# Two blocks of experts and attention on one core: expert chunks cut in halves, value groups without a product of zeros, and a new table of stages

## The reference

```
# block 1
nx = layer_norm(x)                                  # [2,512,128]
w  = softmax(nx @ Wq @ (ctx @ Wk).T * 128**-0.5)    # over 77 context rows
ev = w @ (ctx @ Wv)                                 # "evidence"
comb = concat([nx, ev, cond])                       # 384 wide
p  = softmax(comb @ router_W + router_b)            # 3 experts
h  = silu(comb @ e_w1 + e_b1)                       # 3 experts x 256
routed = sum_e p[e] * (h[e] @ e_w2[e] + e_b2[e])
g  = sigmoid(silu(comb @ gate_w1 + gate_b1) @ gate_w2 + gate_b2)
x  = x + g * (routed @ out_w + out_b)
# block 2, 16 heads of 8 channels, six vectors of cond modulate it
x = x + gate_msa * (self_attention(modulated layer_norm(x)) @ self_o_w + b)
x = x + cross_attention(layer_norm(x), ctx) @ cross_o_w + b
x = x + gate_mlp * (gelu(modulated layer_norm(x) @ mlp_w1 + b) @ mlp_w2 + b)
```

## Time and profile before

| | |
|---|---|
| median of three runs | 314.41 us (312.88 to 314.87) |
| the profiled execution | 312.69 us, span 310.9 us |
| TensorE busy | 259.0 us, 1804 instructions |
| VectorE busy | 173.3 us |
| ScalarE busy | 148.9 us |
| GpSimd busy | 46.1 us |
| mean granted TensorE clock | 0.912 |

### The profile page before, as it was taken

One profiled execution on the slowest core, in us unless ns is written; L12 is line 12 of the kernel. 1 busy time (PEld: TensorE's weight loads), 2 busy tenths in 40 slices (PEclk: granted clock), 3 DMA queues, 4 the chain that ended last, 5 costly groups with the idle time before them and its releaser, 6 DMA issues.

```text
span 310.9 us, 4809 instructions
## 1 busy us (share of the span) xinstructions
PE 259.0 (83%) x1804; PEld 144.4 (46%) x1804; DVE 173.3 (56%) x387; ACT 148.9 (48%) x274; POOL 46.1 (15%) x58
## 2 busy tenths in 40 slices
PE   3779988988557799897989899899899975778786
PEld 2665647446402343343434434354445543457356
DVE  6744224752894878776977874797432534052221
ACT  1213214443002466764855658648877643524442
POOL 1300391183012800000100001001010002000110
PEclk9999999999955789999999999999999997556759
DMA  6969930006440165100021000300002100300000
GB/s 179 407 100 193 175 64 0 2 28 172 149 134 2 47 173 142 50 4 2 0 61 44 2 6 15 91 4 5 2 2 71 51 3 4 98 3 21 2 0 34
DMA packets 15460, 19.72 MB, mean 63 GB/s; under 512 B 3237, under 2 KB 13477, under 8 KB 14445
## 3 DMA queue, kind: packets, MB, share of 16 engines
q1 hardware_dynamic: 15437, 19.42, 23.6%
HBM read 16.19 MB, written 3.03 MB: 62 GB/s over the span
## 4 chain that ended last, share of the span: by engine, by line
PE 47%; ACT 9%; DVE 9%; issue 4%; POOL 0%; ACTq 0%; DVEq 0%; POOLq 0%
PE ps L1141 42%; ACT region L745 6%; DVE neg_max L1019 3%; PE ps L1414 3%; DVE neg_max L1028 2%; ACT pv_sb L754 1%; PE ps L1169 1%; ACT nT L648 1%; PE ps L1425 1%; DVE normed L844 1%; PE ps L1353 1%; DVE max_parts L1047 1%; ACT L745 0%; POOL rstd L542 0%; DVE max_parts L1045 0%
## 5 line engine op out<-in xcount | busy, mean ns | idle before, releaser
L745 ACT ACTIVATE region<-ps 128x512 f32<-128x512 f32 (+1 forms) x160 | 86.7, 595 | 43.5 <-PE ps L1141 42.2
L1019 DVE TENSOR_REDUCE neg_max<-ps 128x2 f32<-128x1024 f32 x64 | 76.5, 1220 | 23.6 <-PE ps L1141 23.0
L1141 PE MATMUL ps<-k_room,Qs 128*128 128x512 bf16 x128 | 41.1, 412 | 6.5 <-DVE neg_max L1019 5.6
L1141 PE MATMUL ps<-Qs,k_room 128*128 128x256 bf16 x256 | 42.5, 279 | 4.1 <-ACT region L745 2.5
L542 POOL TENSOR_TENSOR rstd<-var_eps,minus_half 128x2 f32<-128x2 f32 (+1 forms) x12 | 9.7, 811 | 211.6 <-DVE var_eps L833 211.6
L1141 PE MATMUL ps<-region,V 128*32 128x256 f32 x512 | 39.5, 390 | 0.0
L1141 PEld LDWEIGHTS ps<-Qs,k_room 128*128 128x128 bf16 x256 | 20.2, 99 | 28.7 <-ACT region L745 17.0
L1141 PEld LDWEIGHTS ps<-k_room,Qs 128*128 128x128 bf16 x128 | 10.9, 102 | 21.4 <-issue 9.8
L678 ACT ACTIVATE region<-ps,hidden_b 128x512 f32<-128x512 f32 x14 | 9.5, 686 | 21.0 <-PE ps L1141 21.0
L1028 DVE TENSOR_REDUCE neg_max<-ps 128x8 f32<-128x616 f32 x16 | 12.2, 794 | 12.7 <-PE ps L1141 12.5
L1141 PEld LDWEIGHTS ps<-region,V 128*32 128x32 f32 x512 | 10.8, 108 | 17.2 <-issue 11.7
(11 more groups left out here) (159 smaller groups left out, 338.0 us busy)
## 6 DMA issues: line engine op xcount, KB each, us to landing
Qs<-q_scr SPq DMA_DIRECT2D x24, 192.0 KB
k_room<-k_scr SPq DMA_DIRECT2D x4, 576.0 KB
k_room<-in_pad SPq DMA_DIRECT2D x2, 896.0 KB
Qs<-in_pad SPq DMA_DIRECT2D x4, 448.0 KB
q_scr<-q_parts SPq DMA_DIRECT2D x8, 192.0 KB, 2.1
region<-in_w_hidden SPq DMA_DIRECT2D x1, 1344.0 KB, 9.4
w_attn<-in_w_attn SPq DMA_DIRECT2D x1, 896.0 KB, 14.1
k_scr<-k_parts SPq DMA_DIRECT2D x2, 384.0 KB, 2.5
```

The costliest lines, as they stand in the source:

```text
L745: nc.scalar.activation(probs[0:rows_, s % UNITS, j0:j0 + CT // 2, :], ps[0:rows_, EXP0 + e % 2, :].rearrange("p (j n) -> p j n", n=TU), AC ...
L1019: nc.vector.tensor_reduce(neg_max[:, b, t, h:h + MH], ps[:, bank:bank + MH, :], axis=AX, op=ALU.max, negate=True).then_inc(max_read, 1)
L1141: return nc.tensor.matmul(out, lhsT, rhs, start=start, stop=stop)
```

## The change

Three edits. First, `hidden_layer` of TensorE becomes two functions and two stages: `hidden_x:b.c` issues the product of the normalized input, `hidden:b.c` adds the evidence. The table places three `hidden_x` of the first sequence around `scores:1`, ahead of the first softmax's normalization. Second, a value group of the self attention has no product of zeros; its first value product (first key tile, first half of the heads) carries the start flag, and all others add. Third, the whole table `ORDER` is new (471 words). A stage `warm` and its function are added, too, but the table has none, and the four counts in `START_WARM` are zero, so no instruction comes of it. The memset of the zeros moves to the front of VectorE's instructions.

```
-scores:0 bias:0 scores_norm:0 scores_T:0 scores:1 evidence:0 bias:1 route:0 route_norm:0 hidden:0.0 scores_norm:1
+scores:0 hidden_x:0.0 scores:1 hidden_x:0.1 scores_norm:0 hidden_x:0.2 scores_T:0 bias:0 scores_norm:1 bias:1
...
+            def keep_warm(bank, n):
+
+                claim(bank)
+                for _ in range(n):
+                    mm(ps[:, bank, :], spread(zero16[:, :]), zero16[:, :].to_broadcast([P, T]))
...
-            def hidden_layer(b, c):
+            def hidden_input(b, c):
                 bank = HID0 + c % 4
+                if c == 0:
+                    pe.wait_ge(hidden_in, 16)
+                    pe.wait_ge(nT_ready, b + 1)
                 claim(bank)
                 mm(ps[:, bank, :], hidden_w(c, 0), nT[b][:, :], stop=False)
+
+            def hidden_evidence(b, c):
+                bank = HID0 + c % 4
+                if c == 0:
+                    pe.wait_ge(ev_ready, b + 1)
                 mm(ps[:, bank, :], hidden_w(c, 1), evT[b], start=False).then_inc(hid_raw, 1)
                 read_by(bank, hid_ready, HC * b + c + 1)
...
                     claim(PVB)
-                    if kind == "self":
-
-                        mm(ps[:, PVB, :], spread(zero16[:, :]), zero16[:, :].to_broadcast([P, T]), stop=False)
...
-                        last = mm(out_, V[b][:, kt, VS * h:VS * h + 32], probs[:, s % UNITS, j, :], start=False,
+                        last = mm(out_, V[b][:, kt, VS * h:VS * h + 32], probs[:, s % UNITS, j, :], start=kt == 0 and r == 0,
                                   stop=final)
```

More of the change, by code:

```diff
@@ new lines @@
+weights:1 hidden:0.4 scores_T:1 expert_bias:0 weights:2 hidden_x:0.5 fold:0 fold:1 hidden_x:0.6 hidden:0.5
+hidden:0.6 evidence:1 route:1 expert:0.0 expert:0.1 gate:0 expert:0.2 expert:0.3 gated:0 hidden_x:1.0 stats:1.0
+add_bias:self.1 hidden:1.0 hidden_x:1.1 hidden:1.1 apply:1.0 hidden_x:1.2 hidden:1.2 hidden_x:1.3 norm_T:1.0 keys:0
+send_keys:0 queries:0 send_queries:0 load_keys:0.0 load_queries:0 hidden_x:1.4 route_norm:1 hidden_x:1.5
+load_keys:0.1 hidden:1.3 load_queries:1 hidden:1.4 hidden_x:1.6 weights:3 values:0 expert_bias:1 hidden:1.5
@@ new lines @@
+hidden:1.6 expert:1.0 context_parts:0 expert:1.1 gate:1 expert:1.2 expert:1.3 gated:1 max:0 max:1 max:2 max:3
+max_split:self.0.0.0 add_bias:self.0 max_T:self.0.0.0 stats:1.1 max:4 apply:1.1 max:5 rows:self.0.0.0 max:6
+norm_T:1.1 max:7 keys:1 max_split:self.0.0.1 max:8 max:9 load_exp:0 exp:self.0.0.0.0 max:10 max_T:self.0.0.1
+send_keys:1 max:11 exp:self.0.0.1.0 values:1 max:12 max:13 weigh:self.0.0.0.0 exp:self.0.0.2.0 rows:self.0.0.1
+max:14 max:15 load_keys:1.0 queries:1 exp:self.0.0.0.1 max:16 exp:self.0.0.3.0 exp:self.0.0.1.1 send_queries:1
@@ L1472, in _ @@
             for stage, n in STAGES:
-                if stage == "scores":
+                if stage == "warm":
+                    keep_warm(n[0], n[1])
+                elif stage == "scores":
                     context_scores(n)
@@ L1482, in _ @@
                     route_scores(n)
+                elif stage == "hidden_x":
+                    hidden_input(*n)
                 elif stage == "hidden":
-                    hidden_layer(*n)
+                    hidden_evidence(*n)
                 elif stage == "weights":
```

86 lines of the change are left out of this document (60 added, 26 removed).

## The result

The change takes **297.67 us** (median of four runs, 296.62 to 300.38) against 313.64 (312.77 to 314.87) for the kernel before in the same rounds: a ratio of 0.957, with a 95% interval of 0.950 to 0.964. The forecast was 299.5 us, the range 294 to 308.5. The profiled execution took 298.44 us, 14.25 less than the one of before. In this document medians and ranges are over every execution, while ratios use only executions within 1.5% of their kernel's fastest, which leaves out, among others, the profiled executions of x6 and x10.

A forecast was written before the change was run, and what follows sets the result against it. Limits by stage: TensorE at a low clock early, VectorE from 84 to 118 us, TensorE from 120 to 260. Terms 5.5 + 0 + 4.9 + 3.0 (D, E) + 0.5 = 13.9 us gave 299.5 us, range 294 to 308.5.

The forecast's parts named there:

- A: The start: half products fill a 1.57 us TensorE gap and the clock rises earlier, near 19 us; 5.5 us gained.
- B: 30 to 84 us: chunks cut in two, some waits removed and others added; 0, with one us either way.
- Rival 1: The clock at the start rises no earlier, 3.9 us of A go: 303.5 us, chance 0.15.
- C: Middle, 84 to 118 us: VectorE's waits before maxima fall from 6.3 to about 1 us; 4.9 us gained.
- Rival 2: The middle becomes bound by TensorE at 1.2 GHz, so C gives 0: 304.5 us, chance 0.15.
- rival 4: Maximum rows come late behind sent keys and queries, holding exps and starving VectorE: 319 us, chance 0.05.
- D: Value groups of the self attention: dropping eight products of zeros saves 8 x 0.21 = 1.7 us.
- E: Paired value stages: 61 runs on TensorE instead of 70, each merge saving 0.24 us, 2.2 us in all.
- Rival 3: A merge of value stages saves nothing, a lone stage's extra 0.14 us being a trace artefact: 301.5 us, chance 0.08.
- rival 5: The loop's new order brings its own ScalarE waits, eating D, E and half of C: 305 us, chance 0.12.
- F: The tail: both norms placed after the last projection, removing waits of 0.91 and 0.96 us; 0.5 us gained.

The follow-up runs named there:

- x6: The change plus products of zeros where TensorE waits in its first 17 us: 296.09 us, ratio 0.934 to the kernel before.
- x10: The change with x6's zeros and nine more between the narrow products at the start: 295.01 us, ratio 0.939 to the kernel before.
- x1: The change with the table's first 39 stages in the old order: 304.17 us, ratio 0.970 to the kernel before.
- x2: The change with 90 middle stages, second sequence's norm transposes to second values' transposes, in the old order: 303.08 us, ratio 0.970 to the kernel before.
- x11: The change with the old order from the second values' transposes on, plus zeros in the tail (x7's) and start (x10's): 291.44 us, ratio 0.930.
- x7: The change plus 51 products of zeros in 14 places of the tail where TensorE waits: 292.78 us, ratio 0.929 to the kernel before.
- x8: The change with the zeros of x6 and x7 and 19 more among the middle's first maxima: 292.30 us, ratio 0.929 to the kernel before.
- x4: The change with the eight products of zeros back in the self attention's value groups: 296.99 us, ratio 0.947 to the kernel before.
- x5: The change with eleven value stages moved behind the next max or exp, 67 runs instead of 61: 297.21 us, ratio 0.947 to the kernel before.
- x3: The change with all stages from the second values' transposes on in the old order, without zeros: 296.03 us, ratio 0.945 to the kernel before.

## Why the prediction was right

The forecast held (299.5 against 297.67), but by terms that missed on both sides. That the total came out so close is luck.

**A and B, to the second gated sum: 5.5 + 0 predicted, 5.55 measured, but not where I put them.** At the first gated sum 5.2 us are gained (58.00 to 52.80), 5.3 by x1. TensorE from the second transposes of the norm to that sum, before and with the change:

```profile
10.90:58.00 47.10, 42.86 (x195) 30.73 (x196) 19.11 (x53) 12.15 (x19) 10.96 (x13) 1.00 0.60 129
```

```profile
10.73:52.80 42.07, 40.45 (x195) 28.40 (x196) 18.13 (x52) 12.04 (x19) 10.96 (x13) 0.92 0.77 139
```

With the same 195 records TensorE is busy for 2.4 us less, which is the clock, and idle for 2.6 us less. Of the idle time the wait for the first softmax gave 0.73 us (1.57 to 0.84). The other 1.9 us come from after 30 us, where TensorE of the kernel before waited 0.40, 0.53 and 0.82 us at 37.06, 39.61 and 44.58 us. With the new order these waits are gone; x1 has them again. That is the stretch of B, for which I had forecast 0. So A's own mechanism was worth about 3.3 us instead of 5.5, and B about 2.2 (1.9, and 0.35 between the two gated sums) instead of 0, beyond its one us either way.

In A the softmax ended where I put it (19.33 us against "about 19.3"). But the clock rose at 16.4 and not at 19, the two halves meant to cover the softmax took half as long, and a wait of 0.84 us remained. Then the clock fell from 23.2 to 30.1 us, which I had not allowed for: three us lost, as x2's and x11's rows show. Rival 1 (no earlier rise) is excluded. In B the final wait went (71.65 us has none), and the wait at the norm grew from 0.21 to 1.01 us, as reckoned.

**C, the middle: 4.9 predicted, 8.7 measured.** This is the term that was mis-sized, beyond its upper end of 6.3. VectorE's waits up to max 16 came out as reckoned, three of 1.0 us in all (0.23, 0.62 and 0.17). To the start of max 17 the gain is 5.9 us (33.89 to 27.99). There the prediction took off 0.4 for an exp that would be done later; the new table has six exps before max 17 where the old one had five. The other 2.8 us lie behind max 17, where I had stopped. There the kernel before took 29.36 us to the cut and the change 26.60; VectorE waited 8.7 us for maxima in the one and 4.5 in the other:

```profile
L1019 DVE TENSOR_REDUCE neg_max<-ps 128x2 f32<-128x1024 f32 x17 | 20.6, 1223 | 8.7 <-PE ps L1141 8.5
```

```profile
L1025 DVE TENSOR_REDUCE neg_max<-ps 128x2 f32<-128x1024 f32 x16 | 18.8, 1218 | 4.5 <-PE ps L1147 4.5
```

(groups by line; the numbers are busy time, mean ns of one, idle time before with its releaser.) x2, without zeros, took 28.81 there, so 2.2 us of it are the order; the rest may be the three zero products. Was it the clock? The low stretches in the middle shrank, too (0.84 to 0.91). With the new order the clock is worth little there: the twelve traces that have it range from 54.87 us at 0.88 (x10) to 53.87 at 0.97 (x7), and x8, with zeros added, took 54.54 at 0.97. No run has the old order with the clock held up, so how much of the order's 8.05 us comes through the clock that it keeps up (0.70 before, 0.82 with the change up to max 17) stays open. Rival 2 (TensorE becomes the bound) and rival 4 (late maximum rows) did not come: no exp waits for a transfer in the middle, the longest wait before an exp is 0.98 us, for ScalarE, and the first exp stands 14.7 us behind the second gated sum. (Before it was 25.2, from 83.37 to 108.62; the forecast's 24.5 counts from the first maximum.)

**D, the zeros: 1.7 predicted, about 1.0 measured** by x4's two stretches. The spread of a stretch is of that size, and the time shows nothing.

**E, the merges: 2.2 predicted, nothing measured.** This is the step that failed. From start to start on TensorE a merge does save what I reckoned (without the 0.10 for entering, which these rows don't show):

```profile
142.67 1.93 PE L1147 MATMUL ps<-region,V 128*32 128x256 f32 x32
144.54 0.61 PE L1147 MATMUL ps<-Qs,k_room 128*128 128x256 bf16 x4
...
146.75 0.64 PE L1147 MATMUL ps<-region,V 128*32 128x256 f32 x8
147.32 0.71 PE L1147 MATMUL ps<-Qs,k_room 128*128 128x256 bf16 x4
```

Four stages take 1.87 us to the next instruction, a lone one 0.57, so each further one costs 0.43 as before. But x5 (six merges undone, four in the loop) is not slower, nor x3 (seven in its loop). Rival 3's result was right for another reason than it gave. The Trainium skill's rule (TensorE: Matmul & The Clock Gate, "Measured speedup vs the span model") gives one set of tiles the time of one product and some 4 ns for each further tile; it says nothing of sets in a row. Applied to each set alike, as the forecast did, it gives the right 0 for the kernel's time; for TensorE's own time the rows disagree, as a lone set takes 0.57 us and each further one 0.43. The saving turned into waits, as x5 shows: 1.2 us less of them for exps with four merges undone. D and E together were 3.0 in the forecast; of that the loop returned 0.46 and the middle some 0.5, and TensorE's busy time from 120 to 260 us fell by 2.65 us, not by 4. Even that is too much: the window holds 22 us of the change's tail and only 8 of the old one, and records are missing. Between the cuts of the loop it fell by about 0.9 us (98.04 in 927 records before, five of them zeros; 97.12 in 924 in x6, with the change's order). The error was to count a stretch in which TensorE is busy for 92% as bound by TensorE alone: the largest of the remaining waits are for ScalarE, and with merges they grow. That is rival 5 in a small form; without its loss.

**F, the tail: +0.5 predicted, -0.5 measured.** The waits were exchanged rather than saved:

```profile
277.71 0.66 PE L1435 MATMUL ps<-ident,pv_sb 128*128 128x128 f32 x4 [0.72 <-ACT pv_sb L760]
...
282.24 0.66 PE L1184 MATMUL ps<-ident,normed 128*128 128x128 f32 x2 [0.71 <-DVE x_sb L1074]
283.56 2.07 PE L1147 MATMUL ps<-nT,w_mlp 128*128 128x256 f32 x4 [0.66 <-ACT nT L654]
285.43 0.63 PE L1184 MATMUL ps<-ident,normed 128*128 128x128 f32 x2
285.86 4.55 PE L1147 MATMUL ps<-nT,w_mlp 128*128 128x256 f32 x12
```

The last expansions follow without a wait, where 0.96 us stood before. The transpose of values waits 0.72 us for its own eviction instead of 0.91 for the norm. In return the first norm now waits in the open, as the forecast said, 0.71 us before its transposes and 0.66 behind them; that price was too low in it. And nearly all of the last twelve records ran at the low clock (0.38 us each), where before the last eight took 1.99 us. The half microsecond itself is within the spread of the tail. Its time is a matter of the clock: 56.6 us at 0.73, 51.1 at 0.97 with more work (x7).

So 3.8 us too little in C stand against 2.5 too much in D and E and 1.0 in F, and 2.2 too much in A against 2.2 too little in B. (A slip that changes nothing: by the forecast's own sum rival 4's time is 320.3 us and not 319.)

## What to carry to other kernels

A table of stages pays where an engine visibly waits for the next piece (VectorE for maxima here), and one has to follow the gain past the last big wait, to the point where both orders have done the same work. Where the bounding engine is busy for 92% and another one releases the rest, a shorter instruction is worth only what a run with it undone shows. Where a stretch is a chain of short dependent steps at a low granted clock, products of zeros in its waits can be worth more than any order: 5.5 us for 51 of them in the tail, nothing to be seen for 19 in the middle, where VectorE sets the pace.
